# Two-layer decoder on one core: slot scores in one rounded pass, slot sums from two rounded parts

## The reference

```python
q = (hs @ Wq.T).reshape(B, T, H, DK)
k = (hs @ Wk.T).reshape(B, T, H, DK)
...
s = hs @ Ws1.T @ Ws2.T + bs2
s = jnp.clip(s, -CLAMP, CLAMP).reshape(B, T, H, M).transpose(0, 2, 1, 3)
z = jax.lax.cumlogsumexp(s, axis=2)
es = jnp.exp(s)
enz = jnp.exp(-z)
...
A = jnp.einsum('bhtd,bhjd->bhtj', q, k) * scale
A = jnp.where(mask, A, 0.0)
ok = enz * jnp.einsum('bhtj,bhjm->bhtm', A, es)
qv = jax.nn.softmax(ok, axis=-1)
W2 = jnp.einsum('bhtm,bhjm->bhtj', qv * enz, es)
W2 = jnp.where(mask, W2, 0.0)
o = jnp.einsum('bhtj,bhjd->bhtd', W2, v)
```

## Time and profile before

| | |
|---|---|
| median of three runs | 1765.73 us (1761.0 to 1766.4) |
| profiled execution | 1762.23 us, its span 1760.4 us |
| TensorE busy | 1624.6 us, 92% |
| VectorE busy | 1283.4 us, 73% |
| ScalarE busy | 840.4 us, 48% |
| GpSimd busy | 554.6 us, 32% |

### The profile page before, as it was taken

The page is one execution under the profiler, slowest core; times in us unless marked ns, Lnnn a source line. Parts: engine busy times, 40 slices in busy tenths (PEclk is TensorE's granted clock), DMA queues, the critical chain, the costliest instruction groups (busy, mean ns, idle before and its releaser), DMA issues.

```text
span 1760.4 us, 51382 instructions
## 1 busy us (share of the span) xinstructions
PE 1624.6 (92%) x21686; PEld 1145.0 (65%) x21686; DVE 1283.4 (73%) x2850; ACT 840.4 (48%) x1372; POOL 554.6 (32%) x949
## 2 busy tenths in 40 slices
PE   6999999999958899998999888998998899999989
PEld 5899999999743455554566555665454466666657
DVE  8877787788586888878898352443467798988954
ACT  3433433433441566556567712442243376776752
POOL 5454544534251222403302031541112123431230
PEclk9999999999988999999999979999999999999999
DMA  4010100110026553352462383562913036764200
GB/s 132 1 49 1 49 13 15 65 33 1 21 74 115 101 140 59 100 102 38 102 122 50 72 325 121 190 206 106 163 37 66 20 65 133 133 106 77 42 2 25
DMA packets 91856, 143.93 MB, mean 82 GB/s; under 512 B 14870, under 2 KB 60123, under 8 KB 91628
## 3 DMA queue, kind: packets, MB, share of 16 engines
q1 hardware_dynamic: 87228, 127.79, 31.6%
q10 hardware_dynamic: 2528, 7.74, 1.3%
q0 software_dynamic: 1872, 5.13, 0.8%
HBM read 109.68 MB, written 32.03 MB: 81 GB/s over the span
## 4 chain that ended last, share of the span: by engine, by line
PE 75%; DVE 14%; issue 4%; ACT 4%; POOL 1%; DMA 1%; another core or an unknown queue 1%; ACTq 0%; SPq 0%; POOLq 0%; DVEq 0%
PE bank L1002 22%; PE bank L1210 8%; PE bank L1959 5%; PE bank L1845 4%; PE bank L1847 4%; PE bank L1846 4%; PE bank L740 3%; PE bank L1978 3%; DVE xa_part_max L1283 3%; PE bank L2406 2%; PE bank L677 2%; DVE shared L1283 2%; PE bank L2421 1%; ACT xa_e L1244 1%; PE bank L704 1%
## 5 line engine op out<-in xcount | busy, mean ns | idle before, releaser
L1283 DVE TENSOR_REDUCE xa_part_max<-bank 128x1 f32<-128x448 f32 (+1 forms) x512 | 266.3, 568 | 22.3 <-PE bank L1002 19.5
L1244 ACT ACTIVATE xa_e<-bank 128x1024 f32<-128x1024 f32 (+1 forms) x208 | 211.7, 1023 | 107.5 <-PE bank L1002 105.9
L1244 ACT ACTIVATE ca_e<-bank 128x1024 f32<-128x1024 f32 (+2 forms) x208 | 197.8, 958 | 75.5 <-PE bank L1002 74.5
L1283 DVE TENSOR_REDUCE shared<-bank 128x1 f32<-128x400 f32 (+1 forms) x384 | 205.5, 570 | 21.3 <-PE bank L1002 18.0
L1002 PE MATMUL bank<-xa_kst,xa_qst 122*32 122x448 bf16 (+1 forms) x2048 | 177.5, 345 | 16.1 <-DVE xa_part_max L1283 7.7
L1210 PE MATMUL bank<-xa_e,xa_vaug 128*17 128x256 f32 (+1 forms) x1664 | 132.2, 383 | 4.7 <-ACT xa_e L1244 2.5
L1002 PE MATMUL bank<-xa_qst,xa_kst 128*32 128x256 bf16 (+1 forms) x3264 | 134.1, 274 | 0.0
L1210 PE MATMUL bank<-ca_e,ca_vaug 128*17 128x256 f32 (+2 forms) x1664 | 124.1, 365 | 7.0 <-issue 4.5
L938 POOL TENSOR_TENSOR gsa_qk<-gsa_qk,gsa_rot 128x512 f32<-128x512 f32 x64 | 81.8, 1278 | 138.1 <-DVE gsa_rot L856 138.1
L1002 PE MATMUL bank<-xa_wkv,shared 128*32 128x256 f32 (+1 forms) x1632 | 111.1, 393 | 5.6 <-DVE xa_r L1659 2.5
L1002 PEld LDWEIGHTS bank<-xa_qst,xa_kst 128*32 128x32 bf16 (+1 forms) x3264 | 92.9, 97 | 30.5 <-issue 3.0
(11 more groups left out here) (406 smaller groups left out, 4149.2 us busy)
## 6 DMA issues: line engine op xcount, KB each, us to landing
xa_kst<-xa_k_parts SPq DMA_DIRECT2D x96, 200.1 KB, 5.6
ca_kst<-ca_k_parts SPq DMA_DIRECT2D x96, 200.1 KB, 5.2
xa_k_parts<-xa_parts SPq DMA_DIRECT2D x24, 400.2 KB, 4.8
ca_k_parts<-moe_ctx_parts SPq DMA_DIRECT2D x8, 1200.8 KB
moe_gu<-in_expert_gate_up SPq DMA_DIRECT2D x8, 1024.0 KB
shared<-in_ctxT_split ACTq DMA_DIRECT2D x4, 1601.0 KB, 9.2
moe_ctxT<-in_ctxT SPq DMA_DIRECT2D x8, 800.5 KB, 8.0
ca_cv<-in_ctx SPq DMA_DIRECT2D x4, 1536.0 KB
```

What stands on the lines that cost most here:

```text
L1244: e.activation(self.e[m % 3][0:rows, :, first:T], banks[m % 2][0:rows].rearrange("p a (h t) -> p (a h) t", t=T)[:, :, first:T], ACT.Exp, s ...
L1283: e.tensor_reduce(top, work[:, 0:hi - lo], AX.X, ALU.max).then_inc(*reduced(t, *step))
```

## The change

Slot scores: `u` is computed into three groups of rows (0, 32, 64) by six matmuls instead of two. ScalarE rounds them: rounded u in rows 0 and 64, and in the middle group the remainder, which VectorE subtracts (new step `u_rest`). Ws2 is loaded three times; its first 64 rows are rounded, and the last group holds its remainder, subtracted once. One fp32r product over 96 rows then holds rounded times rounded plus both remainders; before it was an fp32 product over 128 rows.

Slot sums: from unit 4 on, ScalarE writes the exponential twice, rounded as `es_hi` and full as `es`; GpSimd subtracts them (new step `es_rest`), and the sums take six fp32r matmuls over both parts instead of three fp32 ones. In `turn(m)` the step `cs` now stands behind `a` and `o`, and `es_rest` behind the third `qk`; in turn 15 `cs` stands behind a further `gate`. The first sums still are fp32; the triangular matrix is rounded once by ScalarE. The fills before the list change with the new layout.

```diff
--- before.py
+++ after.py
@@
+        es_hi = sb("es_hi", [P, TB, GM])
...
+        es_rest = sb("es_rest", [P, TB, GM])
...
+        es_rested, SPLIT_SUMS = local("gsa", "es_rest"), B
+        U_PARTS, U_ROWS = (0, 32, 64), 96
+        ws2_raw, u_blank, u_top, u_full, ws2_top = (shared[0:U_ROWS, f:f + w] for f, w in ((0, HEADS * SLOTS), (5 * T, T), (6 * T, T), (7 * T, T), (8 * T, HEADS * SLOTS)))
...
@@ turn(m)
-                    ("scale", m - 3, 1), ("ot", m - 3, 0), ("qk", s + 2), ("gate", p + 1), ("w2", p),
-                    ("ok", s - 1), ("ot", m - 3, 1), ("cs", m), ("a", s), ("o", p),
+                    ("scale", m - 3, 1), ("ot", m - 3, 0), ("qk", s + 2), ("es_rest", m), ("gate", p + 1), ("w2", p),
+                    ("ok", s - 1), ("ot", m - 3, 1), ("a", s), ("o", p), ("cs", m),
@@ gsa_loads
-            e.dma_start(ws2[0:RANK + 1, :], a["Ws2T"]).then_inc(*gsa_in["ws2"]("gsa", by=16))
+            for r in U_PARTS:
+                e.dma_start(ws2_raw[r:r + RANK + 1, :], a["Ws2T"]).then_inc(*gsa_in["ws2"]("gsa", by=16))
...
@@ gsa_pe
                     for c in range(DC):
-                        m = e.matmul(ps[0:RANK, 0:T], ws1[:, c, :], hT[:, c, n * T:(n + 1) * T], start=(c == 0), stop=(c == DC - 1))
+                        for r in U_PARTS:
+                            m = e.matmul(ps[r:r + RANK, 0:T], ws1[:, c, :], hT[:, c, n * T:(n + 1) * T], start=(c == 0), stop=(c == DC - 1), skip_group_check=True)
                     m.then_inc(*u_mm(n))
                 elif kind == "es":
                     g, b = divmod(n, B)
-                    q.wait_ge(u_ready, "u", b)
-                    q.wait_ge(gsa_in["ws2"], "gsa")
+                    q.wait_ge(u_rested, b)
+                    q.wait_ge(ws2_lo, "ws2")
+                    q.wait_ge(ws2_hi, "ws2")
                     for i in range(TB):
-                        m = e.matmul(ps[:, i * GM:(i + 1) * GM], u[b][:, i * P:(i + 1) * P], ws2[:, g * GM:(g + 1) * GM], start=True, stop=True)
+                        m = e.matmul(ps[:, i * GM:(i + 1) * GM], u[b][0:U_ROWS, i * P:(i + 1) * P].bitcast(F32R), ws2[0:U_ROWS, g * GM:(g + 1) * GM].bitcast(F32R),
+                                     start=True, stop=True)
...
+                    parts = [es_hi[:].bitcast(F32R), es_rest[:].bitcast(F32R)]
+                    c_, o_ = causal[:, 0:P].bitcast(F32R), ones.bitcast(F32R)
+                    q.wait_ge(es_rested, n)
+                    for i, p in enumerate(parts):
+                        e.matmul(ps[:, 0:GM], c_, p[:, 0, :], start=(i == 0), stop=(i == 1))
+                    for i, p in enumerate(parts):
+                        e.matmul(ps[:, GM:2 * GM], o_, p[:, 0, :], start=(i == 0), stop=False)
+                        m = e.matmul(ps[:, GM:2 * GM], c_, p[:, 1, :], start=False, stop=(i == 1))
@@ gsa_act
+                        e.copy(ws2_top[64:U_ROWS, :].bitcast(F32R), ws2_raw[64:U_ROWS, :])
+                        e.copy(ws2[0:64, :].bitcast(F32R), ws2_raw[0:64, :]).then_inc(*ws2_hi("ws2"))
+                    else:
+                        q.wait_ge(u_rested, n - 1)
                     q.wait_ge(u_mm, n)
-                    e.copy(u[n][0:RANK, :], home(kind, j)[0:RANK, 0:T]).then_inc(*u_ready(*step))
+                    mid = slice(U_PARTS[1], U_PARTS[1] + RANK)
+                    e.copy(u_full[mid, :], home(kind, j)[mid, 0:T])
+                    for r, to in zip(U_PARTS, (u[n], u_top, u[n])):
+                        m = e.copy(to[r:r + RANK, :].bitcast(F32R), home(kind, j)[r:r + RANK, 0:T])
+                    m.then_inc(*u_ready(*step))
...
                 elif kind == "es":
                     q.wait_ge(clipped, *step)
...
+                    if n >= SPLIT_SUMS:
+                        q.wait_ge(cs_mm, n - 1)
+                        e.activation(es_hi[:].bitcast(F32R), es[n % 2][:], ACT.Exp)
                     e.activation(es[n % 2][:], es[n % 2][:], ACT.Exp).then_inc(*es_ready(n))
@@ gsa_dve
+                if kind == "u_rest":
+                    if n == 0:
+                        q.wait_ge(ws2_hi, "ws2")
+                        e.tensor_tensor(ws2[64:U_ROWS, :].bitcast(F32R), ws2_raw[64:U_ROWS, :], ws2_top[64:U_ROWS, :], ALU.subtract).then_inc(*ws2_lo("ws2"))
+                    mid = slice(U_PARTS[1], U_PARTS[1] + RANK)
+                    q.wait_ge(u_ready, "u", n)
+                    e.tensor_tensor(u[n][mid, :].bitcast(F32R), u_full[mid, :], u_top[mid, :], ALU.subtract).then_inc(*u_rested(n))
@@ gsa_pool
+                elif kind == "es_rest":
+                    q.wait_ge(es_ready, n)
+                    q.wait_ge(cs_mm, n - 1)
+                    e.tensor_tensor(es_rest[:].bitcast(F32R), es[n % 2][:], es_hi[:], ALU.subtract).then_inc(*es_rested(n))
```

## The result

The changed kernel takes 1814.09 us (median of 4 runs, 1812.63 to 1816.49) against 1765.47 us: a ratio of 1.0277, with a 95% interval of 1.0259 to 1.0294. The direction was forecast, the size was not: +48.6 us where some +22 was said, and above the upper end of the range (1801). The profiled execution, of 1812.63 us, has a span of 1810.9 us; that of before has 1760.4, so 50.5 us are to be explained.

The account below looks back on a forecast made before the run. TensorE was taken to set the 28.71 us turn, a loop through VectorE, ScalarE and GpSimd close behind. Turns +13.8, opening +8.5, last turn +2.0: 24.3 us on 1762.2, 1786.5; with the median's offset 1788, range 1772 to 1801.

Parts of the forecast that it names:

- The loop of a turn: Turns 4 to 14: queue places through VectorE, ScalarE and GpSimd set 29.96 us a turn, +1.25 each, +13.8 us in all.
- The stall: Turns 4 to 14: TensorE waits about 2.1 us before `o` for GpSimd's masks of the w2 weights, where it had no wait.
- The rival that the passes win: Whole kernel: masks ready when TensorE comes, so only its savings count, 16.5 us, giving 1749 us; chance 0.10.
- The savings themselves: TensorE, by fewer passes: 0.63 us a turn on slot scores, 0.59 on slot sums, together 1.22 us a turn.
- The reciprocal now stands behind o's two operations: its cover is gone: Turns 4 to 14, VectorE: the sums' reciprocal no longer runs during `o`; next square reduction 11.64 us after `o`, before 10.59.
- the opening: Turns 0 to 3: TensorE waits for `u_rest` on VectorE before the scores, and `u` has more matmuls: +8.5 us, bounds 5 and 12.
- the rival that the clock falls too: Turns 4 to 14: half clock behind the new stalls costs 1.5 us a turn, giving 1804 us; chance 0.10.
- under cover ahead of the first rotation: Before 20 us: weight roundings, two more Ws2T loads and fills hidden by waits for VectorE's norms; uncovered roundings, some 2 us.
- The last turn: Turn 15: `es_rest` ready at 433.9 us, so the work behind starts late: +2 us, bounds 0 and 3.
- such a meeting: Before scores 0: VectorE's two-input subtraction held while GpSimd adds the rotation, up to 1.4 us more.
- Only the loop: Whole kernel: the stalls of turns 0 to 3 are absorbed, leaving 1762.2 + 13.8 + 2, 1778 us; chance 0.19.
- the low bounds with the opening half absorbed: Lower end of the forecast range: all parts at their low bounds, turns 0 to 3 half hidden, given as 1772 us.

Follow-up runs that it names:

- the mended kernels: Changed kernel with remainders on GpSimd, rotation tables loaded first, `u` of turn 3 earlier: with fp32 sums 1761.23 us; with split sums and other steps moved 1768.22 us.

## Why the prediction was right in the turn and wrong in the sum

- **The loop of a turn: right.** 29.96 us was said, 30.07 measured; both halves of it agree within 0.07 us, and the place of `es_rest` (+1.23) and `es_hi` (+0.2) came out at 1.22 and 0.25 in the kernel with `es_rest` behind the masks. The stall was 1.7 us for 2.1. The rival that the passes win fell with it: what the scores save bought nothing in a turn that the loop sets. The savings themselves were put a little high: 0.54 us for the scores where 0.63 was said, and 0.89 us from the first of the six passes to the next product (294.70 to 295.59) where 0.71 was said.
- **"The reciprocal now stands behind o's two operations: its cover is gone": the arithmetic was right, its weight not.** With the sums first again the turn is 30.01 us: the other path is as long.
- **The failing step is the opening, "+8.5 us, bounds 5 and 12": it was 16.9.** The pauses before the scores were near what was said: 2.17, 2.21, 1.54 and 2.59 us, 8.5 in all, where the first was put at 3.1 to 4.5 and the others, with the 0.6 us that was taken off each, at about 2.3, 1.9 and 2.4. What was put at nothing is TensorE's clock: 20 us of its work there ran at 1.2 GHz, 10.0 us lost. It stands under the rival that the clock falls too, which I gave 0.10 and worked out for the turns alone; the argument against it, 27 us without a pause, holds for the changed kernel's turns with pauses of 1.7 us. In the opening there are four pauses in 60 us, of 1.5 to 2.6 us, and half clock behind three of them, besides the late rise at 29.6 us. The second thing left out is the sine table, which I had put under cover ahead of the first rotation: 1.2 us late, and with it a longer pause and the clock rose later in this execution. Moving the remainders to GpSimd gave back 12 us of the opening; the tables first and `u` of turn 3 earlier gave back the rest (111.43 us), with no half clock behind 22 us in the mended kernels.
- **"The last turn: +2, bounds 0 and 3": some 8.** The pause was 3.34 us, and TensorE ran at 0.50 for the ten microseconds behind it:

```profile
471.38 0.55 PE L666 MATMUL bank<-gsa_es_hi,gsa_causal 128*128 128x256 f32 x1 [3.34 <-POOL gsa_es_rest L989]
```

  Over the eight profiles with split last sums the time from scores 15 to the end is 1338.9 to 1349.4 us, mean 1345.0; over the six without, 1332.3 to 1342.4, mean 1336.7. So about 8 us are this step's, and the rest of the +13.1 is the spread of that part from one execution to the next.
- **Not seen at all: the two long turns, +5 us (2.0 and 2.95 beyond the others).** The sum costed each instruction by its own duration. But the turn's new length moved GpSimd's weight subtraction beside VectorE's softmax subtraction, 2.0 us in each of the two, and the second paid 0.94 more at half clock. The prediction did weigh such a meeting, for the remainder of Ws2T; there it didn't happen in the changed kernel (1.31 us) and happened in the one with the tables first (2.17).
- **Two sums of the prediction don't add up.** "Only the loop" is 1778 without the 3.5 us from the profiled execution to the median that "The passes win" has; with them it is 1781.5. And the low bounds with the opening half absorbed give 1779.8, not 1772. Neither touches the step that failed.

## What to carry to other kernels

A loop through several engines' queues is costed well by adding up the places in the queues, and an instruction that costs a whole 1.2 us a turn in one place costs nothing in the next. A pause of TensorE can cost more than its length: take what stands behind it at half clock into the sum, above all where pauses come close together or reach 2 us. When a change lengthens the turn, look also at which two-input VectorE operations will now lie beside GpSimd's long ones.

## What the runs showed of the hardware

- Behind every pause of 3.0 us before `o` in the kernel with `es_rest` twice, TensorE's clock was at half for 3 to 7 us. Behind pauses of 3.3 us before the last sums it was at half for ten microseconds in two kernels (as changed, tables first), for some 3.5 us in two (key weights at the turn's end, sums first), and not at all in two (`es_rest` behind the masks, remainders on GpSimd). The last of these:

```profile
458.92 0.36 PE L666 MATMUL bank<-gsa_es_hi,gsa_causal 128*128 128x256 f32 x1 [3.34 <-POOL gsa_es_rest L992]
```

```profile
458.90:464.00 5.10, 5.08 (x42) 4.82 (x43) 3.98 (x3) 2.04 (x5) 1.70 (x4) 1.00 0.00 0
```

- With pauses of 2.0 us before the sums six of ten turns had the half clock and were longer by 1.4 us or more. With pauses of 1.7 us before `o` it fell in two turns of one kernel, and in none of the changed kernel's. So the pause's length alone doesn't tell it; what else does, these runs don't show.
- A VectorE operation of 0.69 us with both inputs in SBUF took 2.80 us beside a GpSimd subtraction of 2.38 us and ended 0.55 us after it, so it looks held until that ended. With the GpSimd subtraction moved away the longest of the sixteen took 0.88. Operations with one input in PSUM kept their 0.69 us beside the same subtraction.
- A 32x1024 subtraction takes 1.31 us on VectorE and 2.37 on GpSimd, a 16x256 one 0.41 and 0.72. On the engine that had time, and earlier in its queue, the slower ones made the kernel 12 us faster.
- Six matmuls in three column groups took 1.05 us where two took 1.04 (`u` of turn 3): they ran beside each other.
